# Graph attention on one core: the attention values of a graph computed one behind the other, other projections around the scores, block transposes of two heads, edge masks and reciprocal root on GpSimd

## The reference, cut to what matters

```python
q = split_heads(x @ Wq + bq); k = split_heads(x @ Wk + bk); v = split_heads(x @ Wv + bv)
scores = einsum('bhqd,bhkd->bhqk', q, k) / sqrt(32) + beta * adj
scores = where(adj > 0, scores, -9e15)
out = einsum('bhqk,bhkd->bhqd', softmax(scores), v)
y = x + merge_heads(out)
result = (y - mean(y)) / sqrt(var(y) + 1e-5)
```

## Time and profile before

| | |
|---|---|
| median of 3 runs | 625.36 us (624.70 to 625.64) |
| the profiled execution | 624.76 us |
| its span | 622.9 us, 20663 instructions |
| TensorE (PE) matmul busy | 602.4 us, 97% |
| VectorE (DVE) busy | 592.3 us, 95% |
| ScalarE (ACT) busy | 576.9 us, 93% |
| GpSimd (POOL) busy | 401.7 us, 64% |
| granted TensorE clock | 0.991 of full speed on average |

### The profile page before, as it was taken

How to read it: one execution, slowest core, us unless ns; L and a number is a source line. 1 busy time by engine, 2 the same in 40 slices (tenths; PEclk the granted TensorE clock), 3 DMA queues, 4 the chain that set the end, 5 groups by cost and what they waited for, 6 DMA issues and landing times. The chain is left out here.

```text
span 622.9 us, 20663 instructions
## 1 busy us (share of the span) xinstructions
PE 602.4 (97%) x6080; PEld 488.5 (78%) x6080; DVE 592.3 (95%) x2266; ACT 576.9 (93%) x2063; POOL 401.7 (64%) x639
## 2 busy tenths in 40 slices
PE   7899999999999999999999999999999999999991
PEld 7887878787878888787878787888878787878850
DVE  4989999999999999999999999999999999999885
ACT  4899999999999999999999999999999999999981
POOL 1333327667767767776766776776777676677664
PEclk9999999999999999999999999999999999999996
DMA  6248889888889988888998888998888898887832
GB/s 195 85 104 193 182 170 229 187 200 203 196 202 204 223 183 202 200 202 195 223 195 197 198 201 198 205 223 182 202 203 201 196 224 189 200 202 172 191 94 102
DMA packets 56190, 117.61 MB, mean 189 GB/s; under 512 B 10512, under 2 KB 12304, under 8 KB 56080
## 3 DMA queue, kind: packets, MB, share of 16 engines
q1 hardware_dynamic: 54992, 116.10, 80.2%
q10 hardware_dynamic: 1088, 0.20, 0.2%
HBM read 22.94 MB, written 12.58 MB: 57 GB/s over the span
## 5 line engine op out<-in xcount | busy, mean ns | idle before, releaser
L521 ACT ACTIVATE probs<-neg_scores,neg_max 128x256 f32<-128x256 f32 x768 | 382.3, 503 | 5.1 <-DVE neg_max L603 1.4
L603 DVE CUSTOM_DVE_ANT_0 neg_scores<-s_bank,bias_sb 128x256 f32<-128x256 f32 x768 | 279.8, 415 | 9.8 <-PE s_bank L466 6.9
L638 DVE STREAM_TRANSPOSE blocks<-probs 128x512 f32<-128x512 f32 x308 | 196.8, 686 | 0.0
L521 ACT ACTIVATION_READ_ACCUMULATOR probs<-neg_scores,neg_max 128x1 f32 x768 | 149.5, 195 | 0.0
L847 POOL TENSOR_SCALAR adj_sb<-adj_sb,beta_col 128x512 f32<-128x512 f32 x31 | 62.2, 2008 | 81.4 <-DVE bias_sb L651 81.4
L466 PE MATMUL s_bank<-qk 32*128 32x256 f32 x1536 | 110.0, 400 | 2.4 <-DVE neg_max L603 1.8
L390 PE MATMUL j_bank<-xt_high,w_high 128*128 128x256 f32 x567 | 110.5, 303 | 0.4 <-DVE xt_low L619 0.3
L537 ACT ACTIVATE qk<-j_bank,qk_bias 128x256 f32<-128x256 f32 x192 | 90.0, 470 | 17.3 <-PE j_bank L390 15.6
L466 PEld LDWEIGHTS s_bank<-qk 32*128 32x128 f32 x1536 | 69.4, 184 | 42.5 <-ACT qk L537 13.3
L889 POOL TENSOR_SCALAR att<-att,rstd,shift 128x384 f32<-128x384 f32 x58 | 95.6, 1656 | 6.3 <-POOL shift L886 6.3
L419 PE MATMUL j_bank<-shuffled,v_sb 128*32 128x256 f32 x1232 | 98.1, 385 | 0.2 <-ACT blocks L533 0.2
(11 more groups left out here) (82 smaller groups left out, 867.3 us busy)
## 6 DMA issues: line engine op xcount, KB each, us to landing
shuffled<-blocks SPq DMA_DIRECT2D x480, 160.0 KB, 4.1
x_sb<-in_x_dram SPq DMA_DIRECT2D x32, 384.0 KB, 6.1
out_dram<-att SPq DMA_DIRECT2D x30, 384.0 KB, 3.4
adj_sb<-in_adj_dram SPq DMA_DIRECT2D x32, 256.0 KB, 6.1
shuffled<-blocks SPq DMA_DIRECT2D x16, 128.0 KB, 2.6
blocks<-in_L_gnn_Wq_dram SPq DMA_DIRECT2D x1, 576.0 KB, 5.8
blocks<-in_L_gnn_Wk_dram SPq DMA_DIRECT2D x1, 576.0 KB, 8.0
blocks<-in_L_gnn_Wv_dram SPq DMA_DIRECT2D x1, 576.0 KB, 5.3
```

The source lines that it names most:

```text
L521: nc.scalar.activation(probs[:, (T * s + t) % (T * NX), :], neg_scores[:, (T * s + t) % (T * NH), :], ACT.Exp, bias=neg_max[:, n % 2, t, h ...
L603: nc.vector.tensor_tensor_reduce(neg_scores[:, (T * s + t) % (T * NH), :], s_bank[h % J][:, t * N:(t + 1) * N], bias_sb[:, n % 2, t, :], - ...
L638: nc.vector.transpose(blocks[:, n % 2, :, h, :, :].rearrange("p k t q -> p t k q"), probs[:, slot:slot + T, :].rearrange("p t (k q) -> p t ...
```

## The change

In steady state (graphs 1 to 30) the jobs of each step are rearranged: the three O jobs of a graph stand at steps 2, 3 and 4 with nothing between them but a step's border, the G jobs at steps 5, 6 and 9, all K and Q jobs ahead of the third scores and both V jobs behind them. VectorE turns two heads in one instruction at steps 0, 3, 4, 7 and 8. The mask of the non-edges of graphs 2 and later is written by GpSimd at the start of `bias`. The chain of the reciprocal root on GpSimd is written with two-operand instructions for each half of the rows. `probs` holds 6 heads, `v_sb` 3 graphs and `heads_t` 3 jobs. The last graph's jobs and the closing work of VectorE have another order. `maxima`, `take`, `run`, `scores` and `exps` are as before.

```diff
-    NX = 5
+    NX = 6
+    TURNS = ((0, 1), (2, 3), (4, 5), (6, 7), (8, 9))
-    CHAIN = 4 * NEWTON + 2
+    CHAIN = 2 * T * NEWTON + 3
         elif n < B - 1:
             jobs = {
-                0: (("O", 0, n - 2),),
                 1: (("X", 0, n + 2), ("K", 0, n + 1)),
-                2: (("G", 0, n - 2), ("Q", 0, n + 1)),
-                3: (("K", 1, n + 1),),
-                4: (("O", 1, n - 2),),
-                5: (("X", 1, n + 2), ("Q", 1, n + 1)),
-                6: (("G", 1, n - 2), ("Q", 2, n + 1)),
-                7: (("V", 0, n + 1),),
-                8: (("O", 2, n - 2),),
-                9: (("X", 2, n + 2), ("K", 2, n + 1)),
-                10: (("G", 2, n - 2),),
+                2: (("Q", 0, n + 1), ("O", 0, n - 2)),
+                3: (("O", 1, n - 2),),
+                4: (("O", 2, n - 2),),
+                5: (("X", 1, n + 2), ("G", 0, n - 2), ("Q", 1, n + 1)),
+                6: (("G", 1, n - 2), ("K", 1, n + 1), ("Q", 2, n + 1)),
+                7: (("K", 2, n + 1),),
+                9: (("X", 2, n + 2), ("G", 2, n - 2), ("V", 0, n + 1)),
                 11: (("V", 1, n + 1),),
             }
         else:
             jobs = {
-                0: (("O", 0, n - 2),),
-                1: (("O", 1, n - 2),),
-                2: (("G", 0, n - 2), ("O", 2, n - 2)),
-                3: (("G", 1, n - 2),),
-                4: (("G", 2, n - 2),),
-                5: (("O", 0, n),),
-                7: (("G", 0, n), ("O", 0, n - 1)),
-                8: (("O", 1, n - 1),),
-                9: (("G", 0, n - 1), ("O", 2, n - 1)),
-                10: (("G", 1, n - 1), ("O", 1, n)),
-                11: (("G", 2, n - 1),),
+                2: (("O", 0, n - 2),),
+                3: (("O", 1, n - 2),),
+                4: (("O", 2, n - 2),),
+                5: (("G", 0, n - 2),),
+                6: (("G", 1, n - 2), ("O", 0, n)),
+                7: (("G", 2, n - 2), ("G", 0, n)),
+                8: (("O", 0, n - 1), ("O", 1, n - 1), ("O", 2, n - 1)),
+                9: (("G", 0, n - 1), ("G", 1, n - 1), ("O", 1, n)),
+                10: (("G", 2, n - 1), ("G", 1, n)),
             }
-    last_jobs = (("O", 2, B - 1), ("G", 1, B - 1), ("G", 2, B - 1))
+    last_jobs = (("O", 2, B - 1), ("G", 2, B - 1))
...
-            def turn_blocks(n, h):
+            def turn_blocks(n, heads):
-                slot = T * (H * n + h) % (T * NX)
-                nc.vector.transpose(blocks[:, n % 2, :, h, :, :].rearrange("p k t q -> p t k q"),
+                slot, rows = T * (H * n + first) % (T * NX), T * len(heads)
+                nc.vector.transpose(blocks[:, n % 2, :, first:last + 1, :, :].rearrange("p k h t q -> p (h t) k q"),
...
-                    if h % J == 0:
-                        turned_now = (h,)
-                    elif h % J == 3 and h < HV:
-                        turned_now = (h - 2, h - 1, h)
+                    if h % J == 0 and by_blocks(n, h):
+                        turn_blocks(n, (h, h + 1))
+                    elif h % J == 3 and by_blocks(n, h):
+                        turn_blocks(n, (h - 1, h))
...
-                    if h == 11 and n + 2 < B:
-                        edges(n + 2)
...
             def bias(n):
+                if n >= 2:
+                    pool.wait_ge(adj_in, (n + 1) * DMA)
+                    pool.wait_ge(max_ready, T * H * (n - 1))
+                    take_wait()
+                    nc.gpsimd.tensor_scalar(key_order(bias_sb[:, n % 2, :, :]), by_keys(adj_sb[:, :, :]), 0.0, MASKED,
+                                            ALU.is_le, ALU.mult).then_inc(not_edge_ready, 1)
...
                 for _ in range(NEWTON):
-                    link(nc.gpsimd.tensor_tensor(nt_a[:, :], rstd[:, :], rstd[:, :], ALU.mult))
-                    link(nc.gpsimd.tensor_tensor(nt_b[:, :], nt_a[:, :], var_eps[:, :], ALU.mult))
-                    link(nc.gpsimd.tensor_scalar(nt_c[:, :], nt_b[:, :], -0.5, 1.5, ALU.mult, ALU.add))
-                    link(nc.gpsimd.tensor_tensor(rstd[:, :], rstd[:, :], nt_c[:, :], ALU.mult))
+                    for t in range(T):
+                        linked(rstd_at[t])
+                        b_at[t] = link(nc.gpsimd.tensor_scalar(nt_b[:, t:t + 1], var_eps[:, t:t + 1], rstd[:, t:t + 1],
+                                                               rstd[:, t:t + 1], ALU.mult, ALU.mult))
+                    for t in range(T):
+                        linked(b_at[t])
+                        rstd_at[t] = link(nc.gpsimd.tensor_scalar(rstd[:, t:t + 1], nt_b[:, t:t + 1], 1.5, rstd[:, t:t + 1],
+                                                                  ALU.add, ALU.mult))
```

More of the change, by code:

```diff
@@ L43, in graph_attention_program @@
     NH = 4
-    NX = 5
+    NX = 6
+    TURNS = ((0, 1), (2, 3), (4, 5), (6, 7), (8, 9))
+    turn_of = {h: i for i, heads in enumerate(TURNS) for h in heads}
     XB = 6
@@ L68, in jobs_of @@
             jobs = {
+                0: (("K", 2, 0),),
                 1: (("K", 0, 1),),
[L70 removed]
+                2: (("Q", 0, 1),),
                 3: (("K", 1, 1),),
@@ L115, in graph_attention_program @@
     second_jobs = (("K", 1, 0),) + tuple(("X", c, 1) for c in range(C))
-    last_jobs = (("O", 2, B - 1), ("G", 1, B - 1), ("G", 2, B - 1))
+    last_jobs = (("O", 2, B - 1), ("G", 2, B - 1))
     ring = [*first_jobs, *second_jobs, *(job for n in range(B) for h in range(H) for job in jobs_of(n, h)), *last_jobs]
     place = {job: r for r, job in enumerate(ring)}
[L121 to L126, removed]
+    heads_slot = {job[1:]: i % 3 for i, job in enumerate([job for job in ring if job[0] == "O"])}
     def on_act(job):
@@ L301, in wait_probs_free @@
                 if by_blocks(before // H, before % H):
-                    wait(eng, blocks_ready, before + 1 - turned_before[before])
+                    wait(eng, blocks_ready, len(TURNS) * (before // H) + turn_of[before % H] + 1)
                 else:
@@ L324, in shuffle @@
                 heads = block_heads(n)
-                sp.wait_ge(blocks_ready, HV * n + heads)
+                sp.wait_ge(blocks_ready, len(TURNS) * n + turn_of[heads - 1] + 1)
                 if n >= 2:
@@ L418, in values @@
                                 probs_k = probs_k.rearrange("p (t a q) -> p a t q", t=T, a=J)
-                        mm = pe.matmul(b[HD * j:HD * (j + 1), 0:N], v_sb[:, n % 4, k, h * HD:(h + 1) * HD],
+                        mm = pe.matmul(b[HD * j:HD * (j + 1), 0:N], v_sb[:, n % 3, k, h * HD:(h + 1) * HD],
                                        probs_k, start=(k == 0), stop=(k == T - 1))
@@ L630, in take @@
                 ins.then_inc(taken_v, 1)
-            def turn_blocks(n, h):
-                dve.wait_ge(exp_ready, T * (H * n + h + 1))
-                if h == 0 and n >= 2:
+            def turn_blocks(n, heads):
+                first, last = heads[0], heads[-1]
+                dve.wait_ge(exp_ready, T * (H * n + last + 1))
+                if first == 0 and n >= 2:
                     dve.wait_ge(shuffled_in[n % 2], n // 2 * J * J * DMA)
-                slot = T * (H * n + h) % (T * NX)
-                nc.vector.transpose(blocks[:, n % 2, :, h, :, :].rearrange("p k t q -> p t k q"),
-                                    probs[:, slot:slot + T, :].rearrange("p t (k q) -> p t k q", q=HD)).then_inc(blocks_ready, 1)
+                slot, rows = T * (H * n + first) % (T * NX), T * len(heads)
+                nc.vector.transpose(blocks[:, n % 2, :, first:last + 1, :, :].rearrange("p k h t q -> p (h t) k q"),
+                                    probs[:, slot:slot + rows, :].rearrange("p t (k q) -> p t k q", q=HD)).then_inc(blocks_ready, 1)
             def invert(n, g):
@@ L798, in _ @@
                         maxima(s + 4)
-                    if h % J == 0:
-                        turned_now = (h,)
-                    elif h % J == 3 and h < HV:
-                        turned_now = (h - 2, h - 1, h)
[L804 to L808, removed]
+                    if h % J == 3:
+                        for job in jobs_of(n, h):
+                            if job[0] == "G":
+                                take(job)
+                    if h % J == 0 and by_blocks(n, h):
+                        turn_blocks(n, (h, h + 1))
+                    elif h % J == 3 and by_blocks(n, h):
+                        turn_blocks(n, (h - 1, h))
                     if h == 0 and n >= 1:
@@ L814, in _ @@
                         moments(n - 3)
-                    if h == 11 and n + 2 < B:
-                        edges(n + 2)
                     if h % J != 1:
                         for job in jobs_of(n, h):
-                            if h % J != 2 or job[0] not in "TG":
+                            if job[0] not in ("", "", "TG", "G")[h % J]:
                                 take(job)
@@ L870, in link, with linked @@
                     ins.then_inc(chain, 1)
-                    pool.wait_ge(chain, CHAIN * n + step[0])
```

(3 more changed lines are left out.)

34 lines of the change are left out of this document (15 added, 19 removed).

## The result

The changed kernel takes 643.55 us (median of 4 runs, 643.41 to 643.78), the kernel before 625.5 us beside it. The ratio is 1.0289, 95% interval 1.0273 to 1.0305: slower, by 18 us. The prediction said 643.5 us, 630 to 651. The profiled execution has a span of 641.3 us, against 622.9.

The account below looks back on a forecast made before the run. The prediction took TensorE to set the period, 18.37 us a graph. To the profiled 624.76 it added 19.0 for the loop, less 0.5 for O jobs and 0.5 at the end: 642.8, median 643.5 us, range 630 to 651.

Parts of the forecast that it names:

- Three O jobs in a row: TensorE at steps 2 to 4: two exits from column tiles saved, 0.25 us a graph, counting only in the last two graphs.
- K1's hold: TensorE behind the second scores: K1 waits for X1's bank, at least 0.52 us a graph, 0.93 with ScalarE's part.
- The loop: From ScalarE's start of X1 through VectorE, TensorE and ScalarE's queue to its next: 19.05 us, 28 x 0.68 = 19.0 us more.
- both lie off the loop: VectorE's savings from two-head turning (0.4 us a graph) and edges moved off it (0.44): counted as nothing in the sum.
- VectorE has 17.7 of 19.05 and still fits: VectorE's work against the period: even if turning two heads saves nothing, it fits.
- Turning two heads at once: VectorE: five fewer instructions save 0 to 0.75 us a graph, taken as 0.4.
- GpSimd's pass: Mask of the non-edges on GpSimd: 2.01 us, replacing a wait for VectorE of 2.6 us a graph, at no cost.
- The end: Last instructions behind GpSimd's closing chain: shorter chains give 0 to 2 us, taken as 0.5 us of gain.
- Rival 1: VectorE alone holds K1, ScalarE starting X1 within 1.2 us of the second scores' end: period 18.64, 632 us; chance 0.13.
- rival 4: A further hold, such as late VectorE maxima or GpSimd's pass over 6 us: 0.3 a graph more, 652 us; chance 0.07.
- rival 2: Faster: TensorE remains the bound and K1's hold costs nothing, 617 us; chance 0.06.
- Rival 3: Faster: VectorE was the true bound, so the period falls to ScalarE's work, 17.65 us, about 603 us; chance 0.04.

Follow-up runs that it names:

- Run 2: The kernel before with only G0 moved from step 2 to step 5, behind X1: 644.43 us, ratio 1.0318.
- run 8: The changed kernel with G1 moved behind Q2, both heads' maxima ahead of X2 at step 9, and graph 29's last G jobs a step sooner: 617.80 us.
- run 1: The changed kernel with K1 directly behind Q1 and G0, and G1 moved to step 7: 622.42 us, ratio 0.9968 to the kernel before.
- run 3: The changed kernel with VectorE taking X1 and G0 at step 5 between the maxima of heads 8 and 9, not behind both: 642.75 us, ratio 1.0287.
- Runs 4 and 6: Mask of the non-edges put back on VectorE at step 11: 4 in the changed kernel, 651.86 us; 6 on top of run 1, 626.55 us.
- run 7: Run 1 with graph 29's G1 and G2 one step sooner in the last graph: 621.78 us, ratio 0.9950 to the kernel before.

## Why the prediction was right, point by point

**What bounds the kernel before** fits the runs: TensorE's own order, with 0.06 us between X1 and the job that needs its bank. Run 2 shows how near the hold was, as it does nothing but put the claim on X1's bank one projection sooner. In run 8 TensorE's own work is 18.14 - 0.13 = 18.01 us a graph; with the 0.27 of the O jobs that makes 18.28 of the 18.38 before, and where the last 0.1 lies no run shows.

**Three O jobs in a row** came out at the upper bound: run 1 has them, and in the changed kernel's timeline they are 308.65 - 305.92 = 2.73 us from the first O to the second scores, against 3 x 1.00; 0.27 for 0.25. TensorE is not the bound there, so it gives nothing, as said.

**K1's hold** was said to be at least 0.52 and 0.93 with ScalarE's part. In the period shown it is 0.63 at K1 and 2.06 - 1.75 = 0.31 at the first scores. Over the 28 periods it is 0.54 at K1, in most of them 0.51 or 0.52, which is the value for VectorE alone. The rest lies between the third scores and the next first ones, 6.11 us on average where run 8 has 5.67: 0.44. So the total was right, 0.98 for 0.93, and its place was half wrong. (K1's start without a hold, put at 1.65 us behind the scores' end where the sum gives 1.63, is 311.43 - 309.72 = 1.71.)

**The loop** was put at 19.05 us and measured 19.00 on average of 28. Its terms, in one period: from ScalarE's X1 to VectorE's 0.62 (0.40 forecast; VectorE's own maxima end only then), to K1 0.53 (0.56), K1 to the third scores 3.34 (3.39), scores, X2 and G2 1.49 (1.36), V0 1.64 (1.75), to ScalarE 0.20 (0.20), V0's taking and ScalarE's stretch to X1 310.91 - 299.55 = 11.36 (11.39). That is 19.18 in this longer period. ScalarE's stretch, the largest term and the one on which a gap and an O's taking had to be estimated, was within 0.03.

But the first of these terms is not ScalarE's: VectorE's maxima end last before X1, so the loop that closes in the changed kernel is another one. It goes from VectorE's X1 to K1 (0.53), to ScalarE's taking of Q2 (314.45 - 312.06 = 2.39), to its X2 (318.13 - 314.45 = 3.68), to VectorE's X2 (0.41), and from VectorE's X2 without a wait to its next X1 (311.53 - 299.39 = 12.14): 19.15 in this period, 19.00 on average. The loop of the prediction lies just below it, with 18.97 in run 3. That the prediction followed only one of two loops and still had the length is in part luck.

**The step that failed** is "both lie off the loop" on VectorE's savings, and with it "VectorE has 17.7 of 19.05 and still fits". Runs 4 and 6 show that work put back into VectorE's queue lengthens the period, by 0.25 and 0.13 us, so the savings keep VectorE's loop as short as ScalarE's. What failed was to count VectorE's work in a period (17.3 us) and not to follow its waits: 0.79 + 0.69 = 1.48 us for ScalarE, at two places.

**Turning two heads at once**: I took 0.4 us a graph. The kernel before, VectorE's timeline, four heads:

```profile
299.84 2.49 DVE L638 STREAM_TRANSPOSE blocks<-probs 128x512 f32<-128x512 f32 x4
```

The next instruction starts at 302.25, so a head costs 0.60; two heads cost (310.06 - 307.77) / 2 = 1.15 for 1.20, and five such instructions save 0.3. **GpSimd's pass** takes 1.98 us for 2.01, and no wait for it is noted in steady state.

**The end** had the wrong sign: I took 0.5 us of gain, and it is a loss of 1.1. The order of the last graph puts G2 of graph 29 at step 7 instead of 4, and GpSimd, whose chain closes the program, waits 4.99 us for it; with these jobs one step sooner (run 7) 1.0 us comes back. I had weighed the shorter chains and not the moved job. Outside the 28 periods the forecast had a gain of 1.0 us, with the O jobs' exits of the last graphs, and the traces have a loss of 1.1 - 0.3 = 0.8. This error and that of the loop, 19.0 forecast where 28 periods brought 17.6, are of opposite sign. That the forecast is off by less than 0.1 us is luck; that the kernel is some 18 us slower through the hold on X1's bank is not.

**Rivals.** Rival 1 is out with its number, as the period is 19.00 and not 18.64, and run 3 shows that VectorE alone does not set it. Yet its condition was nearly met: ScalarE starts X1 1.19 us behind the scores' end in the period shown (310.91 - 309.72), and K1's hold is its 0.52. What it left out is the 0.44 behind the third scores. That part is the late maxima that rival 4 named, but it comes in place of a part of K1's hold and not on top of it. What taking out the second hold alone would bring in the changed kernel was not run. Rivals 2 and 3 fell with the result; what rival 2 would have given, about 617 us, is near what run 8 gives once the holds are gone. Rival 3 followed the Trainium skill, "Perfetto Trace Analysis", section "Identifying the Most-Contended Engine". Here VectorE's occupancy of 98.9% did not tell what the change would bring. VectorE's work was cut, and the time rose; run 2, which leaves VectorE's work as it was, lost 20 us; and in run 8, with VectorE's work cut and the holds nearly gone, the period stops at 18.14 us, 18.01 of them TensorE's, and does not fall to 17.65. The measurement decides against the rule in this case. VectorE's work is not free either: runs 4 and 6 lose 8.3 and 4.1 us by it. VectorE's savings alone, in the order of the kernel before, were not run.

## What to carry to other kernels

In a kernel whose jobs go round a small ring of PSUM banks, the order of jobs is also an order of releases: for each job find the one a ring's length before it and ask when that one is taken, by the slowest of its takers. Room of 0.06 us cannot be seen in any busy share, and moving a job of 0.14 us put the claim on a bank one projection sooner and cost 3%. When a held engine feeds the others in order, follow the hold round through their queues until it comes back: the loop's length, not the hold's, is the price. Do this for each queue that the hold passes, as here two such loops lay within 0.03 us of each other, and take the average of many periods: one period of 19.15 us stood for 19.00 here, and that alone was 4 us in an expectation.

## What the runs showed of the hardware that I had not expected

TensorE is given as busy for 150.00 of 150.00 us in run 8, though a Q is held for 0.13 us in each graph. The row before it is given as lasting to 318.58 + 0.52 = 319.10, beyond Q2's start at 318.99, so a hold this short leaves no idle time in the rows. Distances between starts show it, shares do not.
